# A two-batch mixer kernel: other order of VectorE's B/C work, four banks for the first tokens, three of four output blocks drained by ScalarE

## What is computed

```python
xn = _layernorm(x, axis=-1)
x = x + _mamba2(xn, ...) + _ffn(xn, ...)
# _mamba2, with H = 128 heads of P = 64, state N = 128, G = 8 groups, chunks of 128 tokens
proj = hidden_states @ in_proj_w.T
gate, hBC, dt = jnp.split(proj, [INTER, INTER + CONV_DIM], axis=-1)
hBC = jax.nn.silu(causal_conv_of_4_taps(hBC) + conv_b)
hs, Bx, Cx = jnp.split(hBC, [INTER, INTER + G * N], axis=-1)
dt = jax.nn.softplus(dt + dt_bias)
Gm = jnp.einsum('bclhn,bcshn->bclsh', Cc, Bc)
Y_diag = jnp.einsum('bclsh,bcshp->bclhp', Gm * Lmat, X)
Y_off = jnp.einsum('bclhn,bchpn->bclhp', Cc, prev_states) * sdo
xg = (Y_diag + Y_off + D_res) * jax.nn.silu(gate)
xr = xr * jax.lax.rsqrt(jnp.mean(xr * xr, axis=-1, keepdims=True) + EPS)   # per group
return (xr * norm_weight) @ out_proj_w.T
# _ffn: x @ W.T + b, plus one of four low-rank products chosen by a softmax over x @ gate_w.T
```

## Time and profile before

| | |
|---|---|
| median of 3 runs | 1664.31 us (1662.31 to 1664.91) |
| the profiled execution | 1666.25 us |
| its span, first to last instruction | 1664.5 us |
| TensorE busy | 1625.2 us (98%), 9638 instructions |
| VectorE busy | 1394.8 us (84%), 2361 instructions |
| ScalarE busy | 1253.7 us (75%), 2474 instructions |
| GpSimd busy | 1130.0 us (68%), 1442 instructions |
| TensorE's share of the chain that ended last | 91% (VectorE 4%, GpSimd 2%, ScalarE 1%) |
| mean granted TensorE clock | 0.994 |
| DMA engines, mean | 127 GB/s |

### The profile page before, as it was taken

One profiled execution on the slowest core, in us unless ns is written; L12 is line 12 of the kernel. 1 busy time (PEld: TensorE's weight loads), 2 busy tenths in 40 slices (PEclk: granted clock), 3 DMA queues, 4 the chain that ended last, 5 costly groups with the idle time before them and its releaser, 6 DMA issues.

```text
span 1664.5 us, 28889 instructions
## 1 busy us (share of the span) xinstructions
PE 1625.2 (98%) x9638; PEld 1357.8 (82%) x9638; DVE 1394.8 (84%) x2361; ACT 1253.7 (75%) x2474; POOL 1130.0 (68%) x1442
## 2 busy tenths in 40 slices
PE   6999999999999999999899999999999999999998
PEld 4778888888888888888777788888888888888886
DVE  6888888888888888888879888888888888888887
ACT  3478788787888787887735787878887887878784
POOL 5237776767776777767653487777677777677674
PEclk9999999999999999999999999999999999999999
DMA  4244444344444344444313444444444444434431
GB/s 156 76 135 130 127 145 133 123 146 126 130 146 129 129 144 132 124 146 125 117 39 114 145 125 132 145 127 129 146 123 133 143 128 130 146 123 134 146 112 59
DMA packets 82307, 212.17 MB, mean 127 GB/s; under 512 B 11120, under 2 KB 27504, under 8 KB 81904
## 3 DMA queue, kind: packets, MB, share of 16 engines
q1 hardware_dynamic: 82160, 210.33, 40.0%
HBM read 207.14 MB, written 3.15 MB: 126 GB/s over the span
## 4 chain that ended last, share of the span: by engine, by line
PE 91%; DVE 4%; POOL 2%; ACT 1%; issue 1%; DMA 0%; SPq 0%; ACTq 0%; DVEq 0%; POOLq 0%
PE bg L583 21%; PE bo L726 21%; PE bt L583 11%; PE bh L583 11%; PE by L778 7%; PE bg L798 6%; PE bh L770 3%; PE bt L770 2%; PE bh L786 2%; PE bt L786 2%; DVE cv L820 1%; PE by L583 1%; PE bo L583 1%; PE bo L640 1%; PE bg L705 1%
## 5 line engine op out<-in xcount | busy, mean ns | idle before, releaser
L549 POOL TENSOR_TENSOR xl<-xg,xh 128x256 fp32r<-128x256 f32 x254 | 291.5, 1169 | 351.5 <-ACT xh L407 350.3
L483 POOL TENSOR_TENSOR wl<-raw,wh 128x256 fp32r<-128x256 f32 x584 | 424.3, 757 | 112.7 <-ACT wh L298 112.7
L311 ACT ACTIVATE mt<-cs_row,cs_tok 128x128 f32<-128x128 f32 x1024 | 324.6, 391 | 0.0
L563 POOL TENSOR_TENSOR wol<-raw_o,woh 128x256 fp32r<-128x256 f32 x256 | 181.4, 730 | 40.9 <-ACT woh L441 40.9
L726 PE MATMUL bo<-woh,xh 128*128 128x512 f32 x512 | 201.8, 394 | 2.1 <-POOL xl L549 2.1
L1034 DVE TENSOR_TENSOR mt<-mt,gt 128x1024 f32<-128x1024 f32 x128 | 202.8, 1584 | 0.4 <-ACT mt L450 0.4
L726 PE MATMUL bo<-woh,xl 128*128 128x512 f32 x512 | 200.9, 392 | 0.0
L726 PE MATMUL bo<-wol,xh 128*128 128x512 f32 x512 | 200.8, 392 | 0.0
L820 DVE SCALAR_TENSOR_TENSOR cv<-bt,par_sb,cv 128x511 f32<-128x511 f32 (+2 forms) x216 | 160.9, 745 | 12.4 <-ACT cv L302 7.3
L820 DVE SCALAR_TENSOR_TENSOR cv<-bh,par_sb,cv 128x511 f32<-128x511 f32 (+2 forms) x216 | 160.9, 745 | 6.7 <-ACT cv L302 1.6
L556 POOL TENSOR_TENSOR sqa<-sqa,sq 128x256 f32<-128x256 f32 x222 | 159.0, 736 | 1.2 <-ACT sq L424 1.2
(11 more groups left out here) (179 smaller groups left out, 3549.1 us busy)
## 6 DMA issues: line engine op xcount, KB each, us to landing
raw<-in_w_step SPq DMA_DIRECT2D x128, 512.0 KB, 3.5
cs_row<-cs_rows SPq DMA_DIRECT2D x128, 512.0 KB, 5.4
raw_o<-in_w_out SPq DMA_DIRECT2D x128, 256.0 KB, 4.0
ec_row<-ec_rows SPq DMA_DIRECT2D x256, 96.0 KB, 4.7
raw<-in_w_bc SPq DMA_DIRECT2D x16, 512.0 KB, 3.5
acc<-in_x SPq DMA_DIRECT2D x4, 512.0 KB, 4.7
cs_row<-in_w_ffn SPq DMA_DIRECT2D x2, 1024.0 KB, 5.9
out_dram<-acc SPq DMA_DIRECT2D x1, 1024.0 KB, 6.2
```

The costliest lines, as they stand in the source:

```text
L311: e = act.activation(mt[:, m % 2, h, chunk(j)], cs_row[:, m % 2, h, chunk(j)], ACT.Relu, bias=cs_tok[:, j, 2 * m + h:2 * m + h + 1], scale ...
L483: e = pool.tensor_tensor(wl[:, n % 2, cols], raw[:, n % 2, cols], wh[:, n % 2, cols].bitcast(F32), ALU.subtract)
L549: e = pool.tensor_tensor(xl[:, u, cols], xg[:, u, cols], xh[:, u, cols].bitcast(F32), ALU.subtract)
L563: e = pool.tensor_tensor(wol[:, 1 - u, cols], raw_o[:, 1 - u, cols], woh[:, 1 - u, cols].bitcast(F32), ALU.subtract)
```

## The change

- Start: TensorE makes 12 products of the identity with itself into `by` as soon as the identity is there. The first batch's tokens go to the four banks `bo0` to `bo3`. The DMAs for dt and for group 0's B and C are issued ahead of the linear layer's weights, and the parameters and biases behind them, with semaphores of their own. ScalarE splits the linear layer's weights ahead of `dt_parts`. GpSimd's two constants (`scale_consts`), for which VectorE waits ahead of `soft_log`, stand behind all splits of the linear layer's weights.
- The series has four middle terms and no longer six.
- The B/C steps: VectorE's order in step g becomes taps of B, silu of the C of group g - 1, mask of group g - 3, taps of C, silu of B. ScalarE's order follows. The low-rank addition (`add_lora`) and `decays` stand at the end of step 1, `decays_to_end` at the end of step 3.
- Batch 1's statistics are spread over slots 52 to 57 and its four norms over slots 60 to 63. Its first token block is turned ahead of the wait for `bg`.
- Of the four output blocks of a group VectorE adds one and ScalarE drains three; GpSimd adds two of these in the same slot and the third in the next.
- In the last slot but one of batch 1, `xd`, `xt` and the mask on `mt` stand ahead of the chain from `yo` to `xg`.

The core of the diff (semaphore renames and counts are left out):

```diff
-SERIES = [1.0 / (2 * k + 1) for k in range(8)]
+SERIES = (1.0, 0.33333333660263703, 0.1999985316596525, 0.14296178997116357, 0.10853287901120869, 0.11612164608329507)
+TOP = len(SERIES) - 1
...
+DVE_BLOCKS = 1
+ACT_BLOCKS = NJ - DVE_BLOCKS
+CONST, SCALED, WARM = 6, 3, 12
...
+        def bank_x(b, j):
+
+            return bo[j] if b == 0 else bank_t[j % 2]
...
+            load_x(0)
+            sp.dma_start(hp[:, :], headpar).then_inc(ld_hp, 16)
             load(dtag(0))
+            load(bc(0, 0))
             for b in range(NB):
                 sp.wait_ge(a_ex, did(b * STEPS - 1))
                 sp.dma_start(raw_f, w_ffn).then_inc(ld_ffn, 16)
                 if b == 0:
-                    load(bc(0, 0))
+                    load_par()
                 load(bc(b, 1))
                 if b == 0:
+                    load_wb()
                     load_x(1)
                 for g in range(2, GROUPS):
...
                     split_hi(bc(0, 0))
+                    split_ffn(0)
                     dt_parts(0)
...
                     last_tap(b * UNITS + 2 * g, 0, bank_b[g % 2])
+                    if g >= 1:
+                        tanh_bc(b, g - 1, 1, bank_c[(g - 1) % 2])
+                    if g >= 3:
+                        take_b(b, g - 3)
                     act.wait_ge(t_c, did(b * GROUPS + g))
                     last_tap(b * UNITS + 2 * g + 1, 1, bank_c[g % 2])
                     split_hi(bc(b, g + 2))
                     if g == 0:
                         act.wait_ge(pe_, b * PRO_PE + PE_UT)
                         act.activation(uT, by[:, :], ACT.Copy).then_inc(pa, 1)
-                    tanh_conv(b * UNITS + 2 * g, 0, bank_b[g % 2])
-                    tanh_conv(b * UNITS + 2 * g + 1, 1, bank_c[g % 2])
-                    if g == 0:
+                    tanh_bc(b, g, 0, bank_b[g % 2])
+                    if g == 2:
                         act.wait_ge(pv, b * PRO_DVE + PRO_DVE_CS)
                         act.activation(ecT, csT, ACT.Exp).then_inc(pa, 1)
                         for c in range(NS):
                             e = act.activation(dec[:, chunk(c)], csT[:, chunk(c)], ACT.Exp, scale=-1.0,
                                                bias=csT[:, P * c + P - 1:P * c + P])
                         e.then_inc(pa, 1)
-                    if g >= 2:
-                        take_b(b, g - 2)
...
-                    pool.wait_ge(ld_const, 96)
-                    scale_consts()
                     split_lo(dtag(0))
-                if b == 0:
                     split_lo(bc(0, 0))
                     split_ffn_lo(0, 0)
                 split_ffn_lo(b, 1)
+                if b == 0:
+                    scale_consts()
...
-                    if m == STEPS - 2 and b + 1 < NB:
+                    if m == STEPS - 4 and b + 1 < NB:
...
+            for i in range(WARM):
+                pe.matmul(by[:, chunk(i % NJ)], ident[:, :], ident[:, :], start=True, stop=True)
...
+                    elif b + 1 < NB and m == STEPS:
+                        turn_tokens(b + 1, 0)
+                        pe.wait_ge(v_off, did(n - 2))
+                        for j in range(1, NJ):
+                            turn_tokens(b + 1, j)
                     elif b + 1 < NB:
                         pe.wait_ge(v_off, did(n - 2))
-                        if m == STEPS:
-                            for j in range(NJ):
-                                turn_tokens(b + 1, j)
-                        else:
-                            project_ag(b + 1)
+                        project_ag(b + 1)
...
-                    for k in range(1, TAPS):
-                        tap(un, 0, bank_b[g % 2], k)
-                    for k in range(1, TAPS):
-                        tap(un + 1, 1, bank_c[g % 2], k)
-                    if g == 1:
-                        decays_to_end(b)
-                        dve.wait_ge(pe_, b * PRO_PE + PE_LORA)
-                        for j in range(NJ):
-                            dve.tensor_tensor(acc[:, b, j, :], bo[j][:, :], acc[:, b, j, :], ALU.add).then_inc(pv, 1)
+                    taps_bc(b, g, 0, bank_b[g % 2])
+                    if g >= 1:
+                        silu_conv(un - 1, 1, bank_c[(g - 1) % 2], ct[:, g - 1, :])
+                    if g >= 3:
+                        mask_scores(b, g - 3)
+                    taps_bc(b, g, 1, bank_c[g % 2])
                     if g >= 2:
                         dve.wait_ge(t_bt, did(b * GROUPS + g - 2))
                     silu_conv(un, 0, bank_b[g % 2], h2[:, g % 2, :])
-                    silu_conv(un + 1, 1, bank_c[g % 2], ct[:, g, :])
-                    if g == 0:
+                    if g == 1:
+                        add_lora(b)
                         decays(b)
-                    if g >= 2:
-                        mask_scores(b, g - 2)
+                    if g == 3:
+                        decays_to_end(b)
+                silu_conv(b * UNITS + 2 * GROUPS - 1, 1, bank_c[(GROUPS - 1) % 2], ct[:, GROUPS - 1, :])
+                mask_scores(b, GROUPS - 3)
...
+                    ahead = m == STEPS and b + 1 == NB
+                    if ahead:
+                        take_tokens()
+                        mask_decays()
+                    if has(m - 2):
+                        y_chain()
+                    if m == STEPS and b + 1 < NB:
+                        token_lo(b + 1, 0)
+                        token_lo(b + 1, 1)
...
+                    if b + 1 < NB and STEPS - 12 <= m < STEPS - 6:
+                        h, part_of = divmod(m - (STEPS - 12), 3)
+                        if part_of < 2:
+                            stats_of(b + 1, 2 * h + part_of)
+                        else:
+                            variance(b + 1, h)
+                    if b + 1 < NB and STEPS - NJ <= m < STEPS:
+                        norm(b + 1, m - (STEPS - NJ))
```

188 lines of the change are left out of this document (108 added, 80 removed).

## The result

| | before | changed |
|---|---|---|
| median of the runs beside each other | 1664.03 us (6 runs, 1662.31 to 1664.91) | 1669.97 us (6 runs, 1669.31 to 1670.76) |
| profiled execution | 1666.25 us | 1669.55 us |
| its span | 1664.5 us | 1667.8 us |
| mean granted clock | 0.994 | 0.994 |

The change makes the kernel slower by 5.9 us: the ratio is 1.0037, 95% interval 1.0024 to 1.0050. The forecast was 1685 us and its range began at 1672, so the direction was right and the size was not.

The account below looks back on a forecast made before the run. TensorE, busy almost throughout the slots and B/C steps, was taken as the bound. Batch 0 +11.7, batch 1 +12.0, join -4.1 and end +1.5 gave +21.1 on 1666.25, less 1.94 for the median: 1685 us, range 1672 to 1696.

Parts of the forecast that it names:

- The loop of the B/C steps: Steps 4 to 7: scores wait for VectorE's moved mask, a step takes 8.7 us, +6.3 us in each batch.
- The clock behind the long wait: Behind the new 5.5 us wait ahead of scores(1), TensorE runs slow: +2.3 us per batch (1.5 to 2.9).
- The clock in steps 4 to 7: B/C steps: 1.9 us idle times make the clock fall in every second step, +3.4 us per batch (0 to 6.8).
- The first rival: B/C steps 4 to 7: the clock stays up, no step runs slow, 1678 us; chance 0.25.
- Elsewhere nothing: Slots at group ends: the third block drained by ScalarE stays hidden and changes no time, 0 us.
- A wait of TensorE in the slots at group ends: Sign listed under "Wrong": TensorE waiting in the slots where a group ends; no size given.
- The heads: Start of each batch up to step 4: step 4 comes 0.7 us later in batch 0, 1.0 in batch 1.
- The warm matmuls at nothing: Head of batch 0: an earlier, perhaps faster dt projection counted as no gain, since another row decides.
- The join: Between the batches: statistics waits go, tokens turn earlier, the slow stretch may go: -4.1 us (-4.8 to -2.5).
- The last slots: End of batch 1: `xg` and ScalarE's state copy come later, a new 3.2 us wait: +1.5 us (0 to 3).
- each rival: Clock up 1678 us (0.25), every step slow 1692 (0.17), faster 1648 (0.07), no effect 1664 (0.03).

## Why the prediction was wrong in size

- **The loop of the B/C steps (+6.3 per batch): right.** 8.72 to 8.76 us per step against 8.7, idle 1.8 against 1.9, each time released by the mask. The run with the old order shows that the order is the cause, and the one with the mask alone moved back that only half of the 21 us hangs on the mask's place.
- **The clock behind the long wait (+2.3 per batch): right.** The wait was 5.32 and 5.28 us against 5.5, and filling it gave 2.4 per batch in the time, 2.5 and 2.7 in the trace.
- **The clock in steps 4 to 7 ("I take every second step: +3.4 per batch"): wrong, 6.8 us.** It never fell there: 1.00 over 38 us, and the same in batch 1 from 896.5 to 921 us. The first rival had this right. That section of the Trainium skill ("TensorE: Matmul & The Clock Gate", "HAM oscillation — how this bites in real kernels") warns of longer idle stretches only, and the trace agrees for these steps, but not for some shorter waits elsewhere (last section). I took the pair of short waits in the earlier trace rows as a pattern, from one case.
- **"Elsewhere nothing": wrong, 9.2 us, the largest single error.** I read the slots from the busy share, 684.46 of 685 us, and concluded that nothing is left to gain. The busy time of a group of matmuls includes what its later members wait for. A slot's length, 11.80 beside 11.17, would have shown it in seven slots of each batch. (Slots 0, 7, 15 and so on are long too, 12.3 and 12.0 us, in both kernels alike.) I looked for cover for the added work of ScalarE and GpSimd, and not for what the work taken from VectorE had been delaying: taps, tanh, ScalarE's copy and the states. "A wait of TensorE in the slots at group ends" was on my list of signs of being wrong, and it is the kernel before that had it.
- **The heads: 0.7 and 1.0 forecast.** Scores(1) came at 67.94 for 69.3, and in batch 1 at 890.68, which with the 2.0 us won by then answers to 892.7 for 891.7. The masked rows of batch 0 came at 38.55 and not 39.4. In the sum, 7.7 for 11.7 and 10.2 for 12.0; without the 3.4 of the clock the forecasts were 8.3 and 8.6, so batch 0 was 0.6 better and batch 1 1.6 worse than that.
- **The warm matmuls at nothing: right**, though I had read the same page of the Trainium skill (Part 1, "What's actually happening": activity releases the throttle) as making them worth up to 2.4 us. The run without them shows no loss.
- **The join (-4.1 for -5.0): right**, the norm's spread giving 3.7. The rest is the slow stretch, which was absent here and which other versions with the same turns had.
- **The last slots (+1.5 for -0.4): wrong, 1.9 us.** The copy of the state was late as forecast (1653.94, behind a wait of 3.4 us), but the product behind it starts 9.57 us after the slot's beginning where it started 9.54 before, since the old order had its own waits there; and the slow stretch that ended the kernel before did not come.

The errors add up: -4.0 - 4.7 - 0.9 - 1.8 - 4.5 - 1.9 = -17.8 from +21.1 is +3.3. The range failed because the missed group ends were in no rival: each rival varied the clock or the mask, and the slots were fixed at zero in all. The clock's 6.8 us alone would have left 1678, inside it. The bounds of the terms were also added up a little wide, 10 to 33 us and not 9 to 34, which changes nothing.

## What to carry to other kernels

Measure a period by the distance between the starts of one instruction that it always has, and look at the odd ones out, before calling a stretch full: a group that counts as busy can hold a wait, which the idle column of the matmuls does not show and that of the weight loads does. When an operation is put behind another of the same engine to help that engine, ask first which loop through other engines closes over it; a silu and a mask of 0.68 us each, moved between two sets of taps, made a step 2 us longer, and the mask back in its place took off only 1.1. When parts of a change work against each other, time them apart: here one part cost some 21 us and the others gave back some 15.
